# SBUF places of the matmul operands in both attentions of a two-block transformer kernel

## The chip, the cores and the metric

The kernel runs on one core of a Trainium2 chip. The metric is the device time in microseconds of one execution, taken as the median over several runs. The profile is one further look at one execution: its span runs from the first to the last instruction.

## The reference

The input is x, 32 sequences of 256 tokens and 256 channels in float32, and one condition vector of 256 a sequence. Two transformer blocks follow one another:

```python
# block 0 (film: scale and shift from cond)
h = film(rmsnorm(x, norm1_w), cond, film1_w, film1_b)
Q, K, V = h @ q_w + q_b, h @ k_w + k_b, h @ v_w + v_b      # one head of 256
x = x + softmax(Q @ K.T * D ** -0.5) @ V @ proj_w + proj_b
h = film(rmsnorm(x, norm2_w), cond, film2_w, film2_b)
x = x + gelu(h @ mlp_w1 + mlp_b1) @ mlp_w2 + mlp_b2          # 256 -> 1024 -> 256
# block 1 (shift, scale, gate from silu(c) @ w_ada + b_ada)
x_mod = ln(x) * (1 + scale_msa) + shift_msa
k, q, v = split(x_mod @ w_qkv)                              # 16 heads of 16
x = x + gate_msa * (attention(q / 16, k, v) @ w_proj + b_proj)
x_mod2 = ln(x) * (1 + scale_mlp) + shift_mlp
x = x + gate_mlp * (gelu(x_mod2 @ w_mlp1 + b_mlp1) @ w_mlp2 + b_mlp2)
```

## The kernel before

Four phases follow one another over all 32 sequences, with x held in SBUF throughout: A (attention of block 0), B (its MLP), C (attention of block 1), D (its MLP). Each phase is a software pipeline over the sequences, two of them a loop round, with the first and the last ones written out. Buffers with two copies are numbered 0 and 1 by the parity of the sequence; the profile leaves these numbers out.

**High and low parts.** Most products are taken on float32r operands in three steps. Every operand is split in a high part (rounded to float32r) and a low part (the rest), and `mm3` (from line 210) issues low times high, high times low and high times high into one accumulation. In the order of its arguments the first of a pair is the stationary operand, loaded as weights, and the second the moving one, which streams through the array. The profile names them the other way round: `bank<-a_h_hi,A_m_lo` moves a_h_hi over the stationary m_lo. Each such matmul has 128 stationary columns and 256 moving ones, both 4 bytes a column in each partition.

**Tokens.** `NormBuffers` (line 244) holds the normalized input of a sequence, transposed: `hi` and `lo`, two buffers of 2048 bytes a partition each. "a_" serves both attentions, "m_" both MLPs. Line 253 places the low ones right behind the high ones. Since both are a multiple of 2048 bytes, high and low start at the same place modulo 512.

**Attention A** (from line 451). For a sequence: the transposes of xhat (T, line 413); q (line 751) with the folded query-key weight m_hi, m_lo stationary and the tokens moving; v (line 762) with the tokens stationary and the folded value-projection weight vp_hi, vp_lo moving; S (scores, line 777) with the folded queries q_hi, q_lo stationary and the tokens moving; pT, the transposes of the probabilities (line 791); AV (line 795) with the transposed probabilities pT_hi, pT_lo stationary and v_hi, v_lo moving. q, v, S and AV are 12 matmuls each. The order on TensorE is set by due times in a table, modulo 16, and is in the steady state v, pT, T, S, AV, q, each task for a sequence of its own.

**Attention C** (from line 1507). q and k (`qk_cm`, line 1625) have weights stationary and tokens moving; v (line 1837) has tokens stationary and wt_v moving; the output projection PR (line 1828) has y_hi, y_lo stationary and wt_proj moving; each is 12 matmuls. Between them stand the scores of 16 heads (S0 to S7, line 1750, for the maxima; ST0 to ST7, line 1788, for exp), the weighted sums AV (line 1806) and transposes (lines 1816 and 1824). Every ST waits for the exp before it on ScalarE (line 1896). The order is again a table of due times.

**MLPs B and D** (from line 1017). up: w1 stationary, tokens moving, 48 matmuls a sequence. down: g (the activated hidden values, split) stationary, w2 moving, 48 matmuls.

**Places.** Tensors are placed by a stack allocator in the order of the calls, from the left end of SBUF upwards, or with side="right" from the right end downwards (the weights of B). The place of everything is thus set by the order of the calls and by unused tensors with names that begin with gap. LO_GAP is 32 elements (128 bytes): it stands between most high parts and their low parts. TOP_GAP (line 34) is the first thing on the right side, and so moves all of that side. `Weight.place` places high and low of a weight next to each other, `place_hi` and `place_lo` one of them. `L1Prep` (line 1353) places the weights of attention C.

Of the kernel before, what the change touches and what calls it, by code (L numbers as in the profile page):

```python
# [20 lines left out]
F32R = mybir.dt.float32r  # L21
# [3 lines left out]
P = 128  # L25
EPS = 1e-6
UNROLL = 2
PEEL = 10
X_FIRST = 4
SMALL = 24  # L30
W2_GAP, W2_SHIFT = 80, 48
Y_GAP = 32
GAP_BACK, GAP_BLOCKS = 4624, 1024
LO_GAP, TOP_GAP = 32, 56


class Seq:
# [61 lines left out]
def build(nc, a, out, mod_dram):  # L99


    NB, S, D = a["x"].shape
    TH, KT = S // P, D // P
# [7 lines left out]
    def allocator(stack, prefix):  # L111
        def sb(name, shape, dt=F32):
            return stack.enter_context(nc.sbuf_tensor(prefix + name, shape, dt))

        def ps(name, shape, dt=F32):
            return stack.enter_context(nc.psum_tensor(prefix + name, shape, dt))

        def sem(name):
            return semaphores.enter_context(nc.semaphore(prefix + name))

        def event(name, per=1, skip=0):


            if name in events:
                old = events[name]
                assert old.per == per
                events[name] = Event(old.sem, per, old.base + (NB - skip) * per)
            else:
                events[name] = Event(semaphores.enter_context(nc.semaphore("e_" + name)), per, -skip * per)
            return events[name]  # L130
        return sb, ps, sem, event

    with semaphores, root:
        sb, ps, sem, event = allocator(root, "")
# [2 lines left out]
        ident = sb("ident", [P, P])  # L137
        bank_pairs = [ps(f"bank{i}", [P, 1024]) for i in range(4)]
        banks = [pair[:, half:half + 512] for pair in bank_pairs for half in (0, 512)]
        small = {n: sb(n + "small", [P, SMALL]) for n in ("a_", "m_")}  # L140
        scale0m = sb("scale0m", [P, KT * NB])
        scale1a, shift1a = sb("scale1a", [P, KT * NB]), sb("shift1a", [P, KT * NB])
        rows = sb("rows", [P, 2 * D])
# [4 lines left out]
        class Weight:  # L148
# [3 lines left out]
            def __init__(self, sb, sem, name, view):  # L152
                self.view, self.t, self.N = view, view.shape[0] // P, view.shape[1]
                self.name, self.raw = name, None
                if sb:
                    self.place(sb)
                self.s_in, self.s_hi, self.s_lo = (sem(name + n) for n in ("_in", "_high", "_low"))
                self.s_read = sem(name + "_read") if name != "w2" else None
# [85 lines left out]
        class NormBuffers:  # L244

            def __init__(self, name):
                self.name = name
                t = small[name]
                self.stat, self.mv = t[:, 0:6 * TH], t[:, 6 * TH:8 * TH]
                self.var, self.msq, self.rstd = (t[:, TH * c:TH * (c + 1)] for c in (8, 9, 10))  # L250
                self.xhat = sb(name + "xhat", [P, TH * D])
                self.hi = [sb(f"{name}h_hi{u}", [P, KT * S], F32R) for u in range(UNROLL)]
                self.lo = [sb(f"{name}h_lo{u}", [P, KT * S], F32R) for u in range(UNROLL)]

        attention_norm, mlp_norm = NormBuffers("a_"), NormBuffers("m_")
        scale1m, consts = sb("scale1m", [P, KT * NB]), sb("consts", [P, 8])
        neghalf, one_rows, zero_col = consts[:, 0:TH], consts[:, TH:TH + 1], consts[:, TH + 1:TH + 2]

        BLOCK, QUADS = 32, P // 32
# [191 lines left out]
        def phase_l0_attention(mlp, start):  # L451
            with ExitStack() as st:
                sb, ps, sem, event = allocator(st, "A_")
# [8 lines left out]
                m_hi = sb("m_hi", [P, KT * D], F32R)  # L462
                sb("gap_mlo", [P, LO_GAP])
                m_lo = sb("m_lo", [P, KT * D], F32R)
                vp_hi, vp_lo = sb("vp_hi", [P, KT * D], F32R), sb("vp_lo", [P, KT * D], F32R)

                condT, actT = sb("condT", [P, KT * NB]), sb("actT", [P, KT * NB])
# [230 lines left out]
                def late_modulation(eng):  # L698
# [9 lines left out]
                        ins = add_bias(eng, pmod, 2 * slot, dst, b, lo, norm_w)  # L708
                    ins.then_inc(s_fix, 1)

                q_hi = sb("q_hi", [P, KT * S], F32R)
                sb("gap_q", [P, LO_GAP])
                q_lo = sb("q_lo", [P, KT * S], F32R)
                sb("gap_v", [P, LO_GAP])
                v_hi = [sb(f"v_hi{u}", [P, TH * D], F32R) for u in range(UNROLL)]
                v_lo = [sb(f"v_lo{u}", [P, TH * D], F32R) for u in range(UNROLL)]
                probs = [sb(f"probs{u}", [P, TH * S]) for u in range(UNROLL)]
# [631 lines left out]
        class L1Prep:  # L1349
# [3 lines left out]
            def __init__(self, sb, sem, sb_tmp, mlp):  # L1353
                self.mlp = mlp
                qkv = a["L1_cond_w_qkv"]
                self.w = {n: Weight(None, sem, n, v) for n, v in (("k", qkv[:, 0:D]), ("q", qkv[:, D:2 * D]),
                                                                ("v", qkv[:, 2 * D:3 * D]), ("proj", a["L1_cond_w_proj"]))}
                for n in "kq":
                    self.w[n].place_lo(sb)
                sb("gap_hi", [P, LO_GAP])  # L1360
                for n in "kq":
                    self.w[n].place_hi(sb)
                for n in ("v", "proj"):
                    self.w[n].place(sb)
                self.bias_q = sb("bias_q", [P, 2 * KT * NB])[:, 0:KT * NB]
                for w in list(self.w.values()) + mlp.w:
                    w.place_raw(sb_tmp)
                self.loaded = {n: mlp.w[0].raw[:, i * KT * D:(i + 1) * KT * D] for i, n in enumerate("qk")}
                self.cv, self.brow, mlp.b2row = (sb_tmp("next_" + n, s) for n, s in (
                    ("cv", [P, KT * NB]), ("brow", [NB, D]), ("b2row", [NB, D])))  # L1370
                sb_tmp("next_rest", [P, 448])
                self.blocks, self.back = sb_tmp("blocks", [P, TH * D]), sb_tmp("back", [P, TH * D])
                self.s_raw = {n: sem("raw_" + n) for n in "qk"}
                self.s_b, self.s_cv, self.s_g, self.s_out = (sem(n) for n in ("b", "cv", "g", "out"))
                self.s_one, self.s_zero = sem("one"), sem("zero")
                self.psum = banks[6]
                self.MLP_COL, self.PROJ_COL = 0, 256
                self.COL = {"v": 0, "q": 2 * NB}
# [774 lines left out]
        with near:  # L2153
            sb_near, sem_near = on_the_right(near, "B_")
            mlp0 = Mlp(0, sb_near, sem_near)
            shift1m = sb_near("shift1m", [P, KT * NB])
            mlp0.w.append(Weight(sb_near, sem_near, "w2", a["L0_cond_mlp_w2"]))
            with ExitStack() as early:
                start = Start(on_the_right(early, "Ap_")[0])
            with ExitStack() as raws:  # L2160
                for w in mlp0.w:
                    w.place_raw(on_the_right(raws, "B_")[0])
                heads["A"] = phase_l0_attention(mlp0, start)
            left = allocator(held, "C_")
            mlp1 = Mlp(1, *allocator(held, "D_")[::2])
            with ExitStack() as temps:
                prep = L1Prep(left[0], left[2], allocator(temps, "N_")[0], mlp1)
                heads["B"] = phase_mlp(mlp0, prep, heads["A"])
# [50 lines left out]
```

## Time and profile before

| | |
|---|---|
| time, three runs | 1575.3 us median (1571.78 to 1576.27) |
| profiled execution | span 1576.2 us, beside the longest of the three runs, 1576.27 |
| TensorE busy | 1528.6 us, 97% |
| VectorE, ScalarE, GpSimd busy | 1307.5, 869.0, 388.4 us |
| phase A | to about 265 us |
| phase B | about 300 to 600 us |
| phase C | about 600 to 1215 us |
| phase D | to the end |

Each matmul has a record with its start and a modelled end; one lasts some 280 ns in the records while the next starts after some 113 to 120 ns, since they are pipelined. So the busy time of TensorE says little of its speed, and the distance between two starts is what to read. The timeline gives starts to 0.01 us; over the 12 matmuls of a task that is about 1 ns a matmul.

### The profile page before, as it was taken

Reading aid. Unit: us, or ns where it says so; the run is one execution under the profiler, and the core shown is the slowest. Engines: PE = TensorE matmul, PEld = TensorE weight load, DVE = VectorE, ACT = ScalarE, POOL = GpSimd, SP = SyncE. Lnnn points to the kernel's source line nnn. Section 1 sums busy time; section 2 is a strip of 40 time slices with the busy share of each in tenths; the row PEclk is TensorE's granted clock in tenths of the full one; section 3 lists DMA queues with packets and bytes.
Section 4 is the critical chain, followed back from the end, with each engine's and each line's share of the span. In section 5 each row is a group of like instructions: output and inputs, shape, how many; then the busy total and the mean of one; then the engine's idle time right before and its main releaser. Section 6 shows DMA issues by size and latency. Waiting matters only on the chain.

```text
span 1576.2 us, 42177 instructions
## 1 busy us (share of the span) xinstructions
PE 1528.6 (97%) x14186; PEld 1373.0 (87%) x14186; DVE 1307.5 (83%) x2950; ACT 869.0 (55%) x1781; POOL 388.4 (25%) x525
## 2 busy tenths in 40 slices
PE   8999999999999998899999999999998999999999
PEld 7999998999999998677777777777775999999999
DVE  4788888777777787799999999999985888888886
ACT  3566664444444453566677766677665344444443
POOL 2343332010000013234344344443323200000000
PEclk9999999999999999899999999999998999999999
DMA  5700001211111111444344444443431233222332
GB/s 156 240 20 20 20 20 56 82 44 47 47 51 42 53 48 56 138 134 140 125 137 143 130 137 129 134 144 128 137 121 53 84 101 97 94 97 93 100 100 68
DMA packets 167665, 148.56 MB, mean 94 GB/s; under 512 B 24529, under 2 KB 146449, under 8 KB 167585
## 3 DMA queue, kind: packets, MB, share of 16 engines
q1 hardware_dynamic: 167424, 147.47, 29.3%
q8 instruction: 48, 0.79, 0.2%
q0 software_dynamic: 160, 0.04, 0.1%
q14 instruction: 33, 0.26, 0.1%
HBM read 62.61 MB, written 32.41 MB: 60 GB/s over the span
## 4 chain that ended last, share of the span: by engine, by line
PE 76%; issue 6%; DVE 5%; SPq 4%; DMA 4%; ACT 4%; DVEq 0%; ACTq 0%; POOL 0%; POOLq 0%
PE bank L216 58%; PE bank L1788 5%; PE bank L1806 4%; PE bank L1750 3%; ACT C_probs L1896 2%; DMA m_h_lo<-turned 2%; SPq L2102 2%; SPq L1690 2%; PE bank L1816 1%; PE bank L413 1%; PE bank L791 1%; DMA turned<-N_blocks 1%; PE bank L486 1%; PE bank L198 1%; DMA N_back<-turned 1%
## 5 line engine op out<-in xcount | busy, mean ns | idle before, releaser
L1896 ACT ACTIVATE C_probs<-bank 128x1024 f32<-128x1024 f32 x256 | 263.0, 1027 | 151.5 <-PE bank L1788 151.2
L1762 DVE TENSOR_REDUCE C_negmax<-bank 128x4 f32<-128x1024 f32 x248 | 303.6, 1224 | 30.4 <-PE bank L1750 24.1
L1127 ACT ACTIVATE D_g<-bank,D_bias 128x256 f32<-128x256 f32 x256 | 107.4, 472 | 198.2 <-PE bank L216 198.2
L1127 ACT ACTIVATE B_g<-bank,B_bias 128x256 f32<-128x256 f32 x256 | 107.4, 471 | 196.9 <-PE bank L216 196.8
L372 POOL TENSOR_TENSOR m_small<-m_small,consts 128x2 f32<-128x2 f32 x64 | 48.0, 750 | 592.0 <-DVE m_small L366 308.0
L1788 PEld LDWEIGHTS bank<-C_qs,C_kx 64*128 64x128 f32 x1024 | 77.9, 186 | 94.2 <-ACT C_probs L1896 61.2
L1788 PE MATMUL bank<-C_qs,C_kx 64*128 64x256 f32 x1024 | 130.3, 332 | 19.9 <-ACT C_probs L1896 19.8
L216 PE MATMUL bank<-B_wt_w_hi,B_g_lo 128*128 128x256 f32 x512 | 143.2, 280 | 3.7 <-DVE B_g_lo L1137 3.4
L216 PE MATMUL bank<-D_wt_w_hi,D_g_lo 128*128 128x256 f32 x512 | 141.8, 277 | 1.5 <-DVE D_g_lo L1137 1.5
L216 PE MATMUL bank<-m_h_hi,D_wt_w_lo 128*128 128x256 f32 x512 | 142.2, 278 | 0.8 <-DVE m_h_lo L432 0.8
L216 PE MATMUL bank<-m_h_hi,D_wt_w_hi 128*128 128x256 f32 x512 | 142.0, 277 | 0.0
L216 PE MATMUL bank<-m_h_lo,D_wt_w_hi 128*128 128x256 f32 x512 | 141.9, 277 | 0.0
L216 PE MATMUL bank<-m_h_hi,B_wt_w_lo 128*128 128x256 f32 x512 | 141.7, 277 | 0.0
L216 PE MATMUL bank<-B_wt_w_lo,B_g_hi 128*128 128x256 f32 x512 | 141.6, 276 | 0.0
L216 PE MATMUL bank<-B_wt_w_hi,B_g_hi 128*128 128x256 f32 x512 | 141.5, 276 | 0.0
L216 PE MATMUL bank<-D_wt_w_lo,D_g_hi 128*128 128x256 f32 x512 | 141.4, 276 | 0.0
L216 PE MATMUL bank<-D_wt_w_hi,D_g_hi 128*128 128x256 f32 x512 | 141.4, 276 | 0.0
L216 PE MATMUL bank<-m_h_lo,B_wt_w_hi 128*128 128x256 f32 x512 | 141.4, 276 | 0.0
L216 PE MATMUL bank<-m_h_hi,B_wt_w_hi 128*128 128x256 f32 x512 | 141.4, 276 | 0.0
L1806 PE MATMUL bank<-C_probs,C_vaug 128*32 128x256 f32 x2048 | 139.2, 390 | 0.0
L1750 PE MATMUL bank<-C_kx,C_qs 64*128 64x256 f32 x1024 | 115.9, 304 | 4.3 <-DVE m_xhat L1762 2.4
L1135 DVE CAST B_g_hi<-B_g 128x512 fp32r<-128x512 f32 x128 | 56.4, 440 | 65.6 <-ACT B_g L1127 65.1
(268 smaller groups left out, 4820.3 us busy)
## 6 DMA issues: line engine op xcount, KB each, us to landing
C_qs<-C_q_hi SPq DMA_DIRECT2D x128, 128.0 KB
C_kx<-C_k_hi SPq DMA_DIRECT2D x128, 128.0 KB, 2.6
C_qs<-C_q_lo SPq DMA_DIRECT2D x64, 128.0 KB
C_kx<-C_k_lo SPq DMA_DIRECT2D x64, 128.0 KB, 2.7
C_gbc<-mod_rows SPq DMA_DIRECT2D x32, 256.0 KB, 3.4
D_gbc<-mod_rows SPq DMA_DIRECT2D x32, 256.0 KB, 3.3
turned<-N_blocks SPq DMA_DIRECT2D x31, 256.0 KB, 2.0
N_back<-turned SPq DMA_DIRECT2D x124, 64.0 KB, 2.0
```

The source lines that it names most:

```text
L198: ins = eng.matmul(psum[:, col:col + NB], w.raw[:, k * w.N + c0:k * w.N + c0 + P], shift[:, k * NB:(k + 1) * NB], start=k == 0, stop=k == ...
L216: last = eng.matmul(out_ap, l, r, start=start and i == 0 and k == 0, stop=stop and i == n - 1 and k == 2, skip_group_check=skip)
L372: self.e_rstd.by(eng.tensor_tensor(self.rstd[:, :], self.var[:, :], neghalf[:, :], ALU.pow))
L1127: ins = eng.activation(o, p, func, bias=per_seq(bias1, 2 * u + d, b))
L1135: e_ghi.by(eng.tensor_copy(g_hi[u][:, :], g[u][:, :]))
L1690: eng.dma_start(half(stacked, b, w, slot), qk[f"{name}_{part}"][:, w * S:(w + 1) * S].bitcast(F32))\
L1750: ins = eng.matmul(spair[:, (e * TH + qh) * S:(e * TH + qh + 1) * S], qs[b.par][rows, t * S + qh:(t + 1) * S:TH], kx[b.par][rows, t * S:(t ...
L1762: e_max.by(eng.tensor_reduce(m4[:, :, :, j], spair[:, :].rearrange("p (e q k) -> p e q k", e=2, q=TH), AX, ALU.max, negate=True))
L1788: ins = eng.matmul(stpair[:, (e * TH + kh) * S:(e * TH + kh + 1) * S], kx[b.par][rows, t * S + kh * P:t * S + (kh + 1) * P], qs[b.par][row ...
L1806: ins = eng.matmul(ybank[32 * j:32 * j + 32, (g % 2) * S:(g % 2 + 1) * S], vaug[b.par][:, v0:v0 + 32], probs[h // 2 % NP][:, p0:p0 + S], s ...
L1896: e_exp.by(eng.activation(probs[t % NP][:, :], stpair[:, :], ACT.Exp, scale=scl))
L2102: eng.dma_start(half(qs, b, w, ROW_MAX)[:, :, quad * n:(quad + 1) * n], mT[w][p0:p0 + 16, :].bitcast(F32)).then_inc(s_md[w][b.par], 16)
```

## The change

Six edits, all on places. The calls that compute, wait or move data stay as they are, and so does their order.

- The small tensor `consts` moves to the front of the norm buffers, and unused tensors of 32 bytes take its old place and one new place: what follows lies 64 bytes further on.
- The low tokens of the attentions are placed before the high ones, in front of m_small.
- TOP_GAP grows from 56 to 168 elements: the right side moves down by 448 bytes.
- Attention A gets 256 bytes ahead of vp_hi, 512 ahead of q_hi, and 256 more ahead of v_hi.
- In attention C wt_v moves from behind wt_q_hi to behind wt_q_lo, with 256 bytes ahead of it; wt_proj comes after wt_q_hi without a gap, with 256 bytes behind it.

```diff
--- before.py
+++ after.py
@@ -31,7 +31,8 @@
 W2_GAP, W2_SHIFT = 80, 48
 Y_GAP = 32
 GAP_BACK, GAP_BLOCKS = 4624, 1024
-LO_GAP, TOP_GAP = 32, 56
+LO_GAP, TOP_GAP = 32, 168
+MOVING_GAP, Q_GAP = 64, 128
 
 
 class Seq:
@@ -137,7 +138,11 @@
         ident = sb("ident", [P, P])
         bank_pairs = [ps(f"bank{i}", [P, 1024]) for i in range(4)]
         banks = [pair[:, half:half + 512] for pair in bank_pairs for half in (0, 512)]
-        small = {n: sb(n + "small", [P, SMALL]) for n in ("a_", "m_")}
+        consts = sb("consts", [P, 8])
+        small = {"a_": sb("a_small", [P, SMALL])}
+        attention_lo = [sb(f"a_h_lo{u}", [P, KT * S], F32R) for u in range(UNROLL)]
+        small["m_"] = sb("m_small", [P, SMALL])
+        sb("gap_small", [P, 8])
         scale0m = sb("scale0m", [P, KT * NB])
         scale1a, shift1a = sb("scale1a", [P, KT * NB]), sb("shift1a", [P, KT * NB])
         rows = sb("rows", [P, 2 * D])
@@ -250,10 +255,12 @@
                 self.var, self.msq, self.rstd = (t[:, TH * c:TH * (c + 1)] for c in (8, 9, 10))
                 self.xhat = sb(name + "xhat", [P, TH * D])
                 self.hi = [sb(f"{name}h_hi{u}", [P, KT * S], F32R) for u in range(UNROLL)]
-                self.lo = [sb(f"{name}h_lo{u}", [P, KT * S], F32R) for u in range(UNROLL)]
+                self.lo = attention_lo if name == "a_" else [
+                    sb(f"{name}h_lo{u}", [P, KT * S], F32R) for u in range(UNROLL)]
 
         attention_norm, mlp_norm = NormBuffers("a_"), NormBuffers("m_")
-        scale1m, consts = sb("scale1m", [P, KT * NB]), sb("consts", [P, 8])
+        scale1m = sb("scale1m", [P, KT * NB])
+        sb("gap_consts", [P, 8])
         neghalf, one_rows, zero_col = consts[:, 0:TH], consts[:, TH:TH + 1], consts[:, TH + 1:TH + 2]
 
         BLOCK, QUADS = 32, P // 32
@@ -462,6 +469,7 @@
                 m_hi = sb("m_hi", [P, KT * D], F32R)
                 sb("gap_mlo", [P, LO_GAP])
                 m_lo = sb("m_lo", [P, KT * D], F32R)
+                sb("gap_vp", [P, MOVING_GAP])
                 vp_hi, vp_lo = sb("vp_hi", [P, KT * D], F32R), sb("vp_lo", [P, KT * D], F32R)
 
                 condT, actT = sb("condT", [P, KT * NB]), sb("actT", [P, KT * NB])
@@ -708,10 +716,11 @@
                         ins = add_bias(eng, pmod, 2 * slot, dst, b, lo, norm_w)
                     ins.then_inc(s_fix, 1)
 
+                sb("gap_qhi", [P, Q_GAP])
                 q_hi = sb("q_hi", [P, KT * S], F32R)
                 sb("gap_q", [P, LO_GAP])
                 q_lo = sb("q_lo", [P, KT * S], F32R)
-                sb("gap_v", [P, LO_GAP])
+                sb("gap_v", [P, LO_GAP + MOVING_GAP])
                 v_hi = [sb(f"v_hi{u}", [P, TH * D], F32R) for u in range(UNROLL)]
                 v_lo = [sb(f"v_lo{u}", [P, TH * D], F32R) for u in range(UNROLL)]
                 probs = [sb(f"probs{u}", [P, TH * S]) for u in range(UNROLL)]
@@ -1357,11 +1366,13 @@
                                                                 ("v", qkv[:, 2 * D:3 * D]), ("proj", a["L1_cond_w_proj"]))}
                 for n in "kq":
                     self.w[n].place_lo(sb)
+                sb("gap_v", [P, MOVING_GAP])
+                self.w["v"].place(sb)
                 sb("gap_hi", [P, LO_GAP])
                 for n in "kq":
                     self.w[n].place_hi(sb)
-                for n in ("v", "proj"):
-                    self.w[n].place(sb)
+                self.w["proj"].place(sb)
+                sb("gap_proj", [P, MOVING_GAP])
                 self.bias_q = sb("bias_q", [P, 2 * KT * NB])[:, 0:KT * NB]
                 for w in list(self.w.values()) + mlp.w:
                     w.place_raw(sb_tmp)
```

## Rows read from the trace of the kernel before

**Rows 1.** The page: span, and busy time of each engine.

```profile
span 1576.2 us, 42177 instructions
PE 1528.6 (97%) x14186; PEld 1373.0 (87%) x14186; DVE 1307.5 (83%) x2950; ACT 869.0 (55%) x1781; POOL 388.4 (25%) x525
```

**Rows 2.** Windows: length, busy us of PE PEld DVE ACT POOL, clock, DMA share, GB/s.

```profile
100.00:200.00 100.00, 100.00 (x860) 99.06 (x859) 88.56 (x248) 68.50 (x185) 33.25 (x47) 1.00 0.07 20
...
400.00:500.00 100.00, 100.00 (x885) 100.00 (x884) 76.85 (x184) 42.60 (x101) 6.20 (x9) 1.00 0.14 47
...
900.00:1000.00 100.00, 98.07 (x1053) 73.53 (x1052) 92.30 (x182) 71.72 (x119) 39.42 (x55) 1.00 0.44 138
```

**Rows 3.** Waits of PE from 100 to 250 us: total us, times, longest.

```profile
PE bank L216 <- DVE A_q_lo L858: 0.6, 1, 0.6
PE bank L791 <- ACT A_probs L840: 0.5, 1, 0.5
```

**Rows 4.** The chain that ended last, in B and D: start us, us, what.

```profile
347.80 204.45 PE bank L216 x1800
...
1230.95 341.37 PE bank L216 x3006
```

**Rows 5.** Timeline of PE in attention A: start us, us, instruction.

```profile
127.93 0.28 PE L216 MATMUL bank<-a_h_lo,A_q_hi 128*128 128x256 f32 x1
...
129.18 0.30 PE L216 MATMUL bank<-A_v_hi,A_pT_lo 128*128 128x256 f32 x1
...
130.61 0.28 PE L216 MATMUL bank<-a_h_hi,A_m_lo 128*128 128x256 f32 x1
...
133.41 0.60 PE L791 MATMUL bank<-ident,A_probs 128*128 128x128 f32 x4
...
134.56 0.28 PE L216 MATMUL bank<-a_h_lo,A_q_hi 128*128 128x256 f32 x1
...
135.82 0.28 PE L216 MATMUL bank<-A_v_hi,A_pT_lo 128*128 128x256 f32 x1
...
137.19 0.28 PE L216 MATMUL bank<-a_h_hi,A_m_lo 128*128 128x256 f32 x1
...
137.66 0.28 PE L216 MATMUL bank<-a_h_lo,A_m_hi 128*128 128x256 f32 x1
...
138.57 0.28 PE L216 MATMUL bank<-A_vp_hi,a_h_lo 128*128 128x256 f32 x1
...
139.99 0.60 PE L791 MATMUL bank<-ident,A_probs 128*128 128x128 f32 x4
140.42 0.60 PE L413 MATMUL bank<-ident,a_xhat 128*128 128x128 f32 x4
```

**Rows 6.** The same in attention C.

```profile
964.03 0.28 PE L216 MATMUL bank<-a_h_lo,C_wt_k_hi 128*128 128x256 f32 x1
...
965.21 0.28 PE L216 MATMUL bank<-a_h_hi,C_wt_k_hi 128*128 128x256 f32 x1
...
968.56 0.28 PE L216 MATMUL bank<-C_wt_v_lo,a_h_hi 128*128 128x256 f32 x1
...
969.86 0.60 PE L1824 MATMUL bank<-ident,C_ytok 128*128 128x128 f32 x4
...
975.64 0.28 PE L216 MATMUL bank<-C_wt_proj_lo,C_y_hi 128*128 128x256 f32 x1
...
976.81 0.28 PE L216 MATMUL bank<-C_wt_proj_hi,C_y_hi 128*128 128x256 f32 x1
```

**Rows 7.** Groups of PE's matmuls by form: count, busy us, mean ns of one.

```profile
L216 PE MATMUL bank<-C_wt_v_hi,a_h_lo 128*128 128x256 f32 x128 | 38.6, 302 | 0.3 <-DVE C_q_lo L1659 0.3
```

**Rows 8.** Waits from 952 to 988.1 us: total us, times, longest.

```profile
PEld bank L1788 <- ACT C_probs L1896: 3.3, 6, 0.8
```

**Rows 9.** The chain that ended last, in C: start us, us, what.

```profile
968.60 1.42 PE bank L216 x12
...
988.62 2.85 DMA m_h_lo<-turned
```

## The prediction

> **What bounds the kernel now.** I read the page first, then the same stretches by engine, then the chain, then single starts. On the page TensorE (PE) is busy for 97% of the span [rows 1]. By stretch, PE is busy for the whole of a 100 us window in the first attention and in the first MLP, and for 98 of 100 us in the second attention, at full granted clock [rows 2]. In the first attention, between 100 and 250 us, PE waits once for DVE (0.6 us) and once for ACT (0.5 us) [rows 3]. So the time of that attention and of the MLPs is a number of matmuls times the distance between two starts. I call that distance the pace. It is what this change could alter, since it adds, removes and reorders no instruction, wait or DMA.
>
> The MLPs give the pace to compare with. The chain shows 1800 matmuls of one line in 204.45 us and 3006 in 341.37 us, both 113.6 ns each [rows 4]. The attentions' projections have the same shape, 128 stationary columns and 256 moving ones. Their paces I take from starts in the timeline [rows 5, 6]:
> - First attention, v (138.57 to 139.99, 12 intervals): 118.3 ns.
> - q (137.19 to 138.57): 115.0 over all, of which the first four intervals (to 137.66) 117.5 and the other eight 113.8. So q opens slowly and then falls into the MLPs' pace.
> - Scores S (134.56 to 135.82, 11 intervals): 114.5; in the sequence before (127.93 to 129.18) 113.6. The attend step AV (135.82 to 137.19): 114.2, but 119.2 in the sequence before (129.18 to 130.61). So a task's pace also hangs on the state in which it is entered.
> - Second attention, v (968.56 to 969.86, 11 intervals): 118.2. k (964.03 to 965.21, 10 intervals): 118.0. The output projection (975.64 to 976.81, 10 intervals): 117.0.
>
> The whole prize: in the first attention the 47 intervals 127.93 to 133.41 take 5.48 us and those from 134.56 to 139.99 take 5.43, against 47 x 113.6 = 5.34. That is 0.115 us a sequence, 3.7 us for 32. In the second, v is 0.05 over, k 0.044, the output projection 0.034 at most and q not better known, say 0.12 together, 3.8 us for 32. No placement can bring more than 7.5 us, 0.5% of the time.
>
> **The change, part by part.** What differs is where operands start. I reduce each start modulo 512 bytes, since every slice used as an operand begins a multiple of 512 after its tensor's start. The starts follow from the declared sizes. I write M for the moving operand and W for the stationary one, and M-W for their distance.
>
> All of the left side moves on by 64 bytes (two added gaps of 32), later by 64 + 256 + 512 + 256 in the first attention and 64 + 256 + 256 in the second. The right side moves down by 448, which is also 64 modulo 512. So in both MLPs each M-W stays: 448 and 320 (up) and 192 and 64 (down) in the first, 192 and 64 in the second. I cost them at 0. A pace 1 ns worse over their 6144 matmuls would be 6 us, but 113.6 holds for all these distances [rows 4], and I know of no row in which a common shift of 64 matters.
>
> *Tokens.* High and low tokens start at the same place before, and 128 apart afterwards: from a_h_lo to a_h_hi there are now 4096 + 96 + 32 + 768 + 4096 bytes = 9088, or 384.
>
> *v projections.* There the tokens are the stationary operand. Before, consecutive weights start at the same place, M-W being 448 in the first attention and 64 in the second, all three products alike. It is the only one of the kernel's 256-column products whose high and low stationary operands coincide; everywhere else they are 128 apart. It is also the only one that is at 118 from its first interval to its last, in both attentions [rows 5, 6]. Afterwards M-W is 192 and 64 with weights 128 apart, as in the MLPs' down step, which runs at 113.6. I take it that v then settles as q does. It does not do so at once. Start places fall in two kinds, M an even and W an odd multiple of 64, or the reverse. The MLPs never change kind; AV to q changes it, and so does q to v, before and after. With four slow intervals as in q, eight of twelve gain 118.3 - 113.6 = 4.7 ns, 38 ns a sequence. Bounds: nothing, and 12 x 4.7 = 56 ns. The two v have 3 x 128 matmuls each [rows 7], 32 sequences: 1.2 us in the first attention (0 to 1.8) and the same on PE in the second.
>
> *q, S, k, q.* Here tokens move, and the three products get M-W 192, 320 and 64, where they had 192, 192, 64 (q), 448, 448, 320 (S) and 448, 448, 64 (both of the second attention). Each of these distances occurs in an MLP at 113.6, but no row has low moving data 128 on from high. Gain at best: what they lack, 3.8 us of the 7.5. Loss at worst: the pace 119.2 of the slow AV on all 48 matmuls a sequence, from 115.3 (q and S together; k and the other q are near it), 3.9 x 1536 = 6.0 us [rows 5]. I take 0, nearest to the four distances that all run well.
>
> *AV and output projection.* AV keeps 192 and 64; the output projection goes from 448 and 320 to 192 and 64. Both pairs run at 113.6 in an MLP: 0, the openings being bounded by 5 intervals x 4.7 ns x 64 = 1.5 us either way.
>
> *Transposes.* Identity stays while xhat, probs, ysb and ytok move by 64, so M-W for xhat and ytok goes from 64 to 0. Now four take 0.43 us, 108 ns each, for probs at another distance [rows 5]. 256 of them at 118 would cost 2.6 us; I take 0, since they stream 128 columns in that time and the matmuls twice as many.
>
> *What of the second attention's share reaches the end.* PE waits there 3.3 us by its weight loads for exp in one 36 us round [rows 8]. The chain of that round runs through one v (968.60, 12 matmuls), but at the other, 18 us later, it lies with the way to the turned tokens' DMA (2.85 us from 988.62) and not with PE [rows 9]. If that part sets the round, the second v's gain is given back as waiting. Half to all of 1.2: I take 0.9.
>
> Sum: 1.2 + 0.9 = 2.1 us. The profiled execution has a span of 1576.2, which lies 0.9 above the median of the three runs (1571.78 to 1576.27), so it is one of the longer ones; the same sum is taken off the median: 1575.3 - 2.1 = 1573.2 us.
>
> A rule that speaks against it: the Trainium skill, TensorE: Matmul & The Clock Gate, Step-by-step: what each phase is for, says that TensorE has two independent SBUF read ports, and that "loading the next tile's weights doesn't steal SBUF read bandwidth from the running matmul". By it places don't matter and the time stays at 1575.3. The trace does not settle it: it has two paces for one shape, which the rule doesn't foresee, but no row shows the same product at two places.
>
> **The rivals.**
> (a) All openings go too, and the attentions run at 113.6 throughout: 7.5 us less, 1567.8. For it: 3006 matmuls in a row keep that pace while up and down alternate [rows 4]. Against: transposes and score matmuls stand between the attentions' tasks, and the two kinds stay mixed.
> (b) Places do nothing, and v is slow by what goes before it: 1575.3. For it: AV's 114.2 and 119.2 at places that differ only by whole multiples of 512. Against: v is slow after q, and after transposes in the second attention, alike.
> (c) Slower: the low tokens as moving data, 128 on, keep q, S, k and q from settling, as the coincidence keeps v. The place is these 1536 matmuls; at 120 ns, 4.7 more than 115.3, it costs 7.2 us, less 2.1 gained in v: 1575.3 + 5.1 = 1580.4. It decides from 116.7 ns on, where 1.4 x 1536 eats the 2.1. For it: nothing else in the kernel has this arrangement, so no row vouches for it. Against: each distance on its own runs well.
>
> **How the numbers follow.** Forecast 0.46, (a) 0.20, (b) 0.15, (c) 0.19. A measurement of this kernel tells about 0.3% (4.7 us) from no change, so faster means under 1570.6 and slower over 1580.0. Faster: nearly all of (a), 0.19, and 0.12 of the forecast's case where S and k settle as well: 0.31. Slower: 0.13 of (c) and 0.02 for the transposes and the MLPs' shift: 0.15. The rest, 0.54, is the same. The range reaches past (a), as the runs scatter by 4.5 us, and past (c): 1567.0 to 1581.0. The likeliest case alone: 1570.5 to 1576.
>
> **What would show it.** In the timeline after, v should open with some four intervals of 118 to 120 ns and go on at 113 to 114 in both attentions: 1.38 us or so from v's first start to the transposes, not 1.42. If v takes 1.42 again, coincidence was not its cause (b). The first attention's q and S must keep 1.38 and 1.26; 1.44 is (c). Both MLPs must keep 113.6. A round of the second attention lasts 36 us and should lose 0.05 to 0.08; if v gets faster there and the round doesn't, exp or the DMA sets it. I am wrong as a whole if the time moves by more than 5 us either way.

## The result and the profile after

| | before | after |
|---|---|---|
| time, median of 20 runs each | 1573.35 us (1570.51 to 1577.26) | 1578.1 us (1574.68 to 1581.26) |
| ratio | | 1.0026, 95% interval 1.0017 to 1.0034 |
| profiled execution, span | 1576.2 us | 1573.2 us |

The change makes the kernel slower by 0.26%, some 4.1 us (2.7 to 5.3; the two medians are 4.75 us apart), where 2.1 us less was forecast. The profiled execution after is one of the shorter ones, the one before one of the longer: the two spans alone would show the wrong sign. What differs between them lies in the first sequences of A and in the last ones of B and C, which scatter by 1 to 3.5 us even between two executions of one kernel (e7 and e14 below: 1.3 us at the first q of A, 3.5 us from the end of A to the first k of C). So the traces are compared by their paces in the steady part.

The page of the changed kernel, span and busy time. Against [rows 1] nothing moves by more than 0.2%.

```profile
span 1573.2 us, 42177 instructions
PE 1528.5 (97%) x14186; PEld 1373.7 (87%) x14186; DVE 1309.6 (83%) x2950; ACT 870.5 (55%) x1781; POOL 388.6 (25%) x525
```

Windows of the changed kernel (columns as in [rows 2]). In the first attention TensorE is just as full and at full clock, but gets through 851 matmuls in 100 us where it had 860, 1.0% fewer; in the MLP it has the same 885, and in the second attention 1052 for 1053.

```profile
100.00:200.00 100.00, 100.00 (x851) 99.09 (x850) 88.06 (x242) 68.03 (x184) 32.82 (x47) 1.00 0.07 20
400.00:500.00 100.00, 100.00 (x885) 100.00 (x884) 77.00 (x184) 42.70 (x102) 6.22 (x9) 1.00 0.14 47
900.00:1000.00 100.00, 98.19 (x1052) 73.66 (x1050) 92.69 (x182) 71.00 (x117) 40.29 (x55) 1.00 0.43 135
```

TensorE's waits of the changed kernel from 100 to 250 us are the same two as in [rows 3], so the missing matmuls aren't waiting for anyone:

```profile
PE bank L221 <- DVE A_q_lo L867: 0.5, 1, 0.5
PE bank L800 <- ACT A_probs L849: 0.5, 1, 0.5
```

Timeline of TensorE in A of the changed kernel (start us, us, instruction), answering [rows 5]: second matmul of S, first of AV, of q, the fifth of q, first of v, then the transposes.

```profile
132.91 0.28 PE L221 MATMUL bank<-a_h_lo,A_q_hi 128*128 128x256 f32 x1
...
134.21 0.28 PE L221 MATMUL bank<-A_v_hi,A_pT_lo 128*128 128x256 f32 x1
...
135.62 0.28 PE L221 MATMUL bank<-a_h_hi,A_m_lo 128*128 128x256 f32 x1
...
136.09 0.28 PE L221 MATMUL bank<-a_h_lo,A_m_hi 128*128 128x256 f32 x1
...
137.03 0.29 PE L221 MATMUL bank<-A_vp_hi,a_h_lo 128*128 128x256 f32 x1
...
138.46 0.49 PE L800 MATMUL bank<-ident,A_probs 128*128 128x128 f32 x3
...
138.89 0.49 PE L420 MATMUL bank<-ident,a_xhat 128*128 128x128 f32 x3
```

S takes 1.30 us for its 11 intervals (118.2 ns; before 114.5), AV 1.41 for 12 (117.5; before 114.2), q 1.41 (117.5; before 115.0) and v 1.43 (119.2; before 118.3). q opens with four intervals in 0.47 us as before, but the other eight take 0.94, 117.5 ns, where they took 113.8. The 47 intervals from S to the transposes take 5.55 us; before it was 5.48 and 5.43.

In C of the changed kernel, answering [rows 6]: k from its second to its last start, v from its second start to the transposes.

```profile
962.52 0.29 PE L221 MATMUL bank<-a_h_lo,C_wt_k_hi 128*128 128x256 f32 x1
...
963.70 0.28 PE L221 MATMUL bank<-a_h_hi,C_wt_k_hi 128*128 128x256 f32 x1
...
967.05 0.28 PE L221 MATMUL bank<-C_wt_v_lo,a_h_hi 128*128 128x256 f32 x1
...
967.41 0.28 PE L221 MATMUL bank<-C_wt_v_lo,a_h_hi 128*128 128x256 f32 x1
...
967.64 0.28 PE L221 MATMUL bank<-C_wt_v_hi,a_h_lo 128*128 128x256 f32 x1
...
968.34 0.49 PE L1835 MATMUL bank<-ident,C_ytok 128*128 128x128 f32 x3
```

k takes 1.18 us for 10 intervals as before. v takes 1.29 us for 11 where it took 1.30: it opens at 120 ns (0.36 us for the three from 967.05) and has 117 in the last six (0.70 us from 967.64).

The chain of the changed kernel in B and D (start us, us, what), answering [rows 4]: 234.64 / 2064 = 113.7 ns and 274.61 / 2418 = 113.6. The MLPs' pace is what it was.

```profile
337.69 234.64 PE bank L221 x2064
...
1294.64 274.61 PE bank L221 x2418
```

**All starts together.** The table is worked out from every start in a trace: the mean distance between two matmuls of one task in ns (those under 150), and in brackets what all of them take over 113.3 ns each, in us for the whole phase. 113.3 is the pace of a task that has settled, as I call it when it has come down and stays there. The step from a task's last matmul to the next task isn't counted. The kernels e1 to e8 are told of below.

```
        before        after         e3 (after)    e1            e2            e7            e8
A q     115.2 (0.64)  117.8 (1.55)  117.8 (1.56)  117.8 (1.55)  115.3 (0.68)  115.2 (0.64)  117.8 (1.55)
A v     117.7 (1.54)  118.0 (1.65)  117.9 (1.58)  118.1 (1.66)  117.8 (1.55)  117.7 (1.55)  118.0 (1.64)
A S     116.5 (1.03)  118.0 (1.49)  118.2 (1.55)  118.1 (1.53)  117.0 (1.20)  116.8 (1.11)  118.1 (1.54)
A AV    115.1 (0.63)  116.6 (1.13)  116.6 (1.13)  116.3 (1.04)  114.7 (0.48)  114.4 (0.39)  116.4 (1.06)
C k     116.7 (1.07)  117.7 (1.38)  117.8 (1.38)  117.7 (1.38)  115.6 (0.73)  115.3 (0.63)  117.7 (1.38)
C q     114.7 (0.45)  117.7 (1.41)  117.8 (1.45)  118.1 (1.53)  116.9 (1.16)  116.6 (1.06)  117.8 (1.45)
C v     117.9 (1.48)  117.2 (1.21)  116.8 (1.09)  115.7 (0.78)  114.5 (0.36)  114.6 (0.40)  116.6 (1.03)
C PR    115.9 (0.81)  115.3 (0.63)  115.7 (0.74)  115.7 (0.74)  115.5 (0.69)  116.2 (0.90)  115.7 (0.74)
sum            7.64         10.45         10.49         10.21          6.84          6.69         10.40
us of 22 sequences in A's loop
        143.64        145.19        145.20        145.10        143.65        143.52        145.17
us of C's loop
        396.55        395.77        396.10        396.37        396.20        395.81        396.98
```

e3 is the changed kernel once more, and repeats its means to 0.4 ns: the paces belong to the kernel and not to the execution. Two executions of e7's kernel (e7 and e14) differ in one task by up to 0.9 ns (C's q, 0.30 us) and in the sum by 0.09 us. C's k and q scatter most: they take 1.07 and 0.45 us before, and 0.76 and 0.87 in e4, which has the same distances. With the last step of each task counted the sums are 8.34 us before and 11.06 after, 2.7 us apart instead of 2.8.

A's loop grows by 1.55 us in 22 sequences; scaled to 32 that is an estimate of 2.25 us. C's loop doesn't grow, though k and q in it do: TensorE isn't what sets a round there [rows 8, 9]. So the traces account for some 2.3 us of the 4.1 (2.7 to 5.3) measured; the second measurement of the same kernel gave 2.5 (0.5 to 4.6). What is left, 0.4 to 3 us, I can't place, because the written-out first and last sequences scatter by more.

### The profile page after: what moved, and what is told of

Read it like the earlier page. It is cut to its first block, busy times and chain, and to the rows that moved or that the text cites. A ratio compares the mean times of both kernels' runs of the same rounds, so it can differ in the third digit from the quotient of the medians.

```text
span 1573.2 us, 42177 instructions
## 1 busy us (share of the span) xinstructions
PE 1528.5 (97%) x14186; PEld 1373.7 (87%) x14186; DVE 1309.6 (83%) x2950; ACT 870.5 (55%) x1781; POOL 388.6 (25%) x525
## 4 chain that ended last, share of the span: by engine, by line
PE 80%; issue 5%; DVE 5%; ACT 4%; DMA 3%; SPq 2%; DVEq 0%; ACTq 0%; POOL 0%; POOLq 0%
PE bank L221 59%; PE bank L1799 6%; PE bank L1817 6%; PE bank L1761 4%; ACT C_probs L1907 2%; PE bank L1827 2%; PE bank L420 1%; PE bank L800 1%; DMA m_h_lo<-turned 1%; PE bank L1835 1%; PE bank L494 1%; SPq L1701 1%; ACT C_y_f L1925 1%; SPq L2113 1%; ACT C_y_hi L1924 1%
```

## The experiments

Each was a change of places alone, unless its diff says otherwise. Distances (a, b, c) are, modulo 512: a, how many bytes further on the high moving operand starts than the high stationary one; b, the low moving one than the high stationary; c, the high moving one than the low stationary.

**Which part costs.** e1 has the changed kernel's tokens, the low ones 128 on, while weights, folded queries and v_hi keep their distances to the high tokens as before; e2 is the changed kernel with the low tokens back at the place of the high ones; e4 is the kernel before with everything moved by 64; e3 is the changed kernel once more.

```diff
 e1, against the changed kernel
-                sb("gap_vp", [P, MOVING_GAP])
-                sb("gap_qhi", [P, Q_GAP])
-                sb("gap_v", [P, LO_GAP + MOVING_GAP])
+                sb("gap_v", [P, LO_GAP])
...
 e2, against the changed kernel
-        attention_lo = [sb(f"a_h_lo{u}", [P, KT * S], F32R) for u in range(UNROLL)]
...
-                self.lo = attention_lo if name == "a_" else [
-                    sb(f"{name}h_lo{u}", [P, KT * S], F32R) for u in range(UNROLL)]
+                self.lo = [sb(f"{name}h_lo{u}", [P, KT * S], F32R) for u in range(UNROLL)]
 e4, against the changed kernel: both of these
```

> Of the change only the low tokens' place (128 on from the high ones) and the common shift of 64; weights, folded queries and value weights keep the distances of before. Theory L (low tokens 128 on as the moving operand keep q, S, k and q from settling): q of the first attention at 118 ns (12 intervals 1.41 us, before 1.38), S at 118, both of the second attention at 118, so it is as slow as the changed kernel, +0.2% on before. Theory D (the distances that the change gave weights and queries do it, 320 for the low tokens on the high weights): q of the first attention has the changed kernel's distances and is at 118, S has 448, 64, 320 and settles at 113 to 114. Theory N (the slowdown is not in TensorE's pace): paces as before, time as before.

> The changed kernel with the low tokens behind the high ones again, at the same place modulo 512. Every product but v then has M-W 192, 192, 64, as the last MLP's. Theory L: q, S, k and q settle at 113 to 114 within the first third of the task, AV is entered settled; v stays at 118 throughout, its stationary operands coinciding. Time 3 to 5 us below the changed kernel, 0 to 2 us below before. Theory D: the distances of weights and queries are kept, so q and S stay at 118 and the time is the changed kernel's. Theory N: no pace changes.

> Before, with everything that holds a matmul operand 64 bytes on modulo 512 and no distance between operands altered (only identity and x stay). Theories L and D: paces of every task as before (first attention q 115, v 118, S 114 to 117, AV 114 to 119), time within 0.15% of before. Theory N (a shift as such costs, or the transposes, whose distance to identity goes to 0): transposes above 109 ns or MLPs above 113.6, and +0.2%.

> The changed kernel unaltered, a second profiled execution. If the paces are a property of the places, q, S, k, q and v show the same interval at the same position of the loop as in the first profile, to 1 ns; if they drift with the execution, the two profiles differ there. Time 0.2 to 0.35% over before.

Measured, with 95% intervals: e1 1.0017 (1.0005 to 1.0029), e2 0.9989 (0.9977 to 1.0001), e4 1.0003 (0.9987 to 1.0018), e3 1.0016 (1.0003 to 1.0029). The low tokens' place carries the slowdown: with it e1's paces in q, S, k and C's q are those of the changed kernel, without it e2's are not, and the intervals of e1 and e2 lie apart. Modulo 512, e1 differs from e4 in this place alone. Timeline of e1: first q, first v.

```profile
128.97 0.28 PE L221 MATMUL bank<-a_h_hi,A_m_lo 128*128 128x256 f32 x1
...
130.38 0.29 PE L221 MATMUL bank<-A_vp_hi,a_h_lo 128*128 128x256 f32 x1
```

The same of e4:

```profile
133.46 0.28 PE L220 MATMUL bank<-a_h_hi,A_m_lo 128*128 128x256 f32 x1
...
134.84 0.28 PE L220 MATMUL bank<-A_vp_hi,a_h_lo 128*128 128x256 f32 x1
```

q takes 1.41 us in e1 and 1.38 in e4 (117.8 and 115.2 ns in the mean over all sequences), though the intervals of the two whole times overlap.

The common shift does nothing that stands clear of the scatter: e4's sum over the eight tasks is 7.53 us, beside 7.64 before. One v of C in e2 (start us, us, instruction; second, fourth, seventh start, transposes):

```profile
946.98 0.28 PE L220 MATMUL bank<-C_wt_v_lo,a_h_hi 128*128 128x256 f32 x1
...
947.22 0.28 PE L220 MATMUL bank<-C_wt_v_hi,a_h_lo 128*128 128x256 f32 x1
...
947.56 0.28 PE L220 MATMUL bank<-C_wt_v_hi,a_h_lo 128*128 128x256 f32 x1
...
948.24 0.49 PE L1833 MATMUL bank<-ident,C_ytok 128*128 128x128 f32 x3
```

From 947.22 to 948.24 it has 9 intervals of 113.3 ns, though its high and low stationary tokens coincide modulo 512 as they do in the kernel before. So coincidence of the stationary operands, the cause that the forecast named, is not enough to keep v slow in C. (The moving operands start 192 on from the coinciding ones here, and 64 before.) Of A's v this says nothing; it runs at 117.8 in e2.

**Late or never?** In e5 (changed) and e6 (before) q, v and S of A are issued three times in a row, 36 matmuls instead of 12, the same result.

```diff
-                        for t in range(KT):
+                        for t in [*range(KT)] * 3:
```

> The changed kernel with the 12 matmuls of q, of v and of S of the first attention each issued three times over into the same bank (36 in a row, the result the same), to see where a task's pace goes if it is given time. Theory L, strong form (low tokens 128 apart as moving data never settle): q and S stay at 118 over all 36, while v, whose distances are those of the MLPs' down step, is at 113 to 114 from about the 12th on. Theory O (the opening is only longer): q and S are at 113 to 114 in their last 12.

> The same threefold issue in the kernel before. Theory V (coincident high and low stationary operands keep v from settling, as my prediction had it): v at 118 over all 36. Theory O: v is at 113 to 114 in its last 12, so that in the kernel before too it only lacked time. q and S at 113 to 114 in the last 24 by either.

Timeline of e5: first q, first v, eighth v, transposes, second S, first AV.

```profile
150.20 0.28 PE L221 MATMUL bank<-a_h_hi,A_m_lo 128*128 128x256 f32 x1
...
154.44 0.28 PE L221 MATMUL bank<-A_vp_hi,a_h_lo 128*128 128x256 f32 x1
...
155.28 0.28 PE L221 MATMUL bank<-A_vp_lo,a_h_hi 128*128 128x256 f32 x1
...
158.57 0.49 PE L800 MATMUL bank<-ident,A_probs 128*128 128x128 f32 x3
...
159.56 0.28 PE L221 MATMUL bank<-a_h_lo,A_q_hi 128*128 128x256 f32 x1
...
163.69 0.28 PE L221 MATMUL bank<-A_v_hi,A_pT_lo 128*128 128x256 f32 x1
```

The same of e6: first q, the fifth, first v, transposes, second S, first AV.

```profile
151.12 0.28 PE L216 MATMUL bank<-a_h_hi,A_m_lo 128*128 128x256 f32 x1
...
151.60 0.28 PE L216 MATMUL bank<-a_h_lo,A_m_hi 128*128 128x256 f32 x1
...
155.23 0.28 PE L216 MATMUL bank<-A_vp_hi,a_h_lo 128*128 128x256 f32 x1
...
159.47 0.49 PE L791 MATMUL bank<-ident,A_probs 128*128 128x128 f32 x3
...
160.47 0.28 PE L216 MATMUL bank<-a_h_lo,A_q_hi 128*128 128x256 f32 x1
...
164.45 0.28 PE L216 MATMUL bank<-A_v_hi,A_pT_lo 128*128 128x256 f32 x1
```

With the low tokens 128 on, 36 matmuls of q take 4.24 us, 117.8 ns each to the end, and S 4.13 us for 35, 118.0. In the kernel before q takes 4.11 us, 0.48 for the first four and 3.63 for the other 32, 113.4 each, and S 3.98, 113.7. v is the reverse: 4.24 us throughout before, 117.8 ns, while after it has 120 ns for seven intervals and then 3.29 us for 29, 113.4. So q and S don't settle late, they don't settle at all; and with the changed places v can settle, here from its eighth interval on. In the changed kernel itself, where v has twelve matmuls and is entered from a shorter q, it doesn't get there: its intervals 8 to 12 are some 118, 120, 118, 114 and 116 ns (medians over the sequences). The whole times, 1831.25 and 1833.39 us, are one run each and tell nothing at this size.

**Which distance of the low tokens?** e7 puts them 256 on, e8 384 on. e14 is e7 again.

```diff
 e7, against the changed kernel
-        attention_lo = [sb(f"a_h_lo{u}", [P, KT * S], F32R) for u in range(UNROLL)]
         small["m_"] = sb("m_small", [P, SMALL])
         sb("gap_small", [P, 8])
+        attention_lo = [sb(f"a_h_lo{u}", [P, KT * S], F32R) for u in range(UNROLL)]
```

> The changed kernel with the low tokens 256 instead of 128 on from the high ones. Theory L (what counts is that high and low moving data start at different places): q, S, k and q of the second attention stay at 118, time as the changed kernel, +0.15 to 0.25% on before. Theory D (what counts is the distance 320 of the low tokens from the high weights, here 448): they settle at 113 to 114, time 3 us below the changed kernel.

> The changed kernel with the low tokens 384 on from the high ones; their distance to the high weights is 64. Theory L: 118 as in the changed kernel. Theory D: 113 to 114 after the opening.

> The changed kernel with the low tokens 256 on instead of 128, once more. By the sum over the tasks 0.95 us under the kernel before; its ten runs so far gave a ratio of 0.9983 (0.9965 to 1.0001). All theories: a ratio between 0.9985 and 1.0; if the interval ends under 1 it beats the kernel before.

Timeline of e7: first q, the fifth, first v.

```profile
134.74 0.28 PE L221 MATMUL bank<-a_h_hi,A_m_lo 128*128 128x256 f32 x1
...
135.22 0.28 PE L221 MATMUL bank<-a_h_lo,A_m_hi 128*128 128x256 f32 x1
...
136.12 0.28 PE L221 MATMUL bank<-A_vp_hi,a_h_lo 128*128 128x256 f32 x1
```

q opens in 0.48 us and has 0.90 for the other eight, 113 ns. In e8 it stays at 117.8. e7 measured 0.9983 (0.9965 to 1.0001), and again 0.9994 (0.9981 to 1.0006); e8 1.0002 (0.9985 to 1.0019), though its paces are those of the changed kernel. So its time alone would not show the slowdown; what counts here is the paces, and A's loop of 145.17 us. Together: with 0 or 256 between the moving high and low tokens A's q and C's k settle in every sequence, while S of A and C's q, at 116.6 to 117.0 ns in the mean, come down late in one sequence of two. With 128 or 384 none of the four settles. So it isn't any difference between the two that does harm, and not the distance 320 alone either (e8 has 64 in its place).

**The moving operands' distance from one another, or from the weights?** e10: low tokens together with the high ones, and the stationary operands of A's q and S moved by 128, distances (64, 64, 448).

```diff
 e10, against e2
+                sb("gap_mhi", [P, 32])
                 m_hi = sb("m_hi", [P, KT * D], F32R)
...
-                sb("gap_qhi", [P, Q_GAP])
+                sb("gap_qhi", [P, Q_GAP + 32])
```

> Low tokens at the place of the high ones modulo 512, as before; in attention A the stationary operands of q and S are moved by 128 bytes, so that high and low moving tokens are each 64 on from the high stationary part (192 before in q, 448 in S), and 448 from the low one. So far q, S, k and q of C did not settle (118 ns over all twelve) wherever the low tokens stood 64 or 320 on from the high stationary part, which was also wherever they stood 128 or 384 from the high tokens. Theory M-M (only the distance of the two moving operands from one another counts): q and S of A settle, 115.2 to 117 ns in the mean, with 113 at the end of q. Theory M-W (64 or 320 from moving to high stationary is what keeps the pace up): q and S of A stay at 118 over all twelve. Attention C is as in the kernel with the low tokens together, in both.

Timeline of e10: first q, first v; second S, first AV.

```profile
128.50 0.28 PE L220 MATMUL bank<-a_h_hi,A_m_lo 128*128 128x256 f32 x1
...
129.91 0.28 PE L220 MATMUL bank<-A_vp_hi,a_h_lo 128*128 128x256 f32 x1
...
138.91 0.28 PE L220 MATMUL bank<-a_h_lo,A_q_hi 128*128 128x256 f32 x1
...
140.16 0.32 PE L220 MATMUL bank<-A_v_hi,A_pT_lo 128*128 128x256 f32 x1
```

q: 1.41 us for 12, 117.5 (mean 118.3 over all sequences). S: 1.25 for 11, 113.6 (114.6). One and the same set of distances, and q never settles while S does at once. Neither theory holds: the moving operands' distance from one another isn't all, and (64, 64, 448) isn't bad by itself.

e13 has these distances in S alone.

> The kernel with the low tokens together with the high ones modulo 512, and q_hi, q_lo alone moved by 128 bytes, so that S of A has the distances 64, 64, 448, while q of A keeps 192, 192, 64. With weights and folded queries both at 64, q ran at 118.3 and S at 114.6 (116.5 in the kernel before, 117.0 with 192). Theory places: S runs at 114.6 here as well, 0.7 to 0.8 us less than with 192, and q at 115.2: a sum over the eight tasks of about 6.1 us over 113.3, 1.5 us under the kernel before, so 1573.8 beside 1575.3. Theory entry (S ran well there since what stands before it was in another state): S stays at 116 to 117, and the sum at 6.8.

S ran at 117.1, 0.2 us slower than in the kernel before over the phase and not faster: in every second sequence it opened 117 116 114 and then stayed at 113 to 114 (medians over the sequences), in the others it went on at 118 with a 124 among them. After an S that has settled AV runs at 113 to 114 from its second interval, after the other kind it stays at 116 to 122 for eight, at the same places. What stands before S decides too, so e10's good S was not its places' doing alone. For q the pair says more: e10 and e13 differ in the place of q's weights alone, and q runs at 118.3 and 115.3. The time was 1572.29 us, ratio 0.9982 (0.9969 to 0.9995): the only kernel whose interval ends below 1. Its sum over 113.3 is 7.01 us, 0.6 less than before, which is a fifth of the 2.8 us that the ratio says, and A's loop takes 144.05 us, 0.4 more than before. So its paces don't explain its time. e7's first ratio moved from 0.9983 to 0.9994 when it was measured again, and e13 was measured once; its gain may be chance.

**Why does v of A stay slow?** e11 is e2 with q, v and S thrice. e9 is e7 with v moved behind the transposes pT, so that it comes out of transposes as in C; e12 is e9 with the PSUM banks of v and S exchanged.

```diff
 e9, against e7 (hi_v and lo_v follow, at 39 and 40.5)
-                T_PE = {"T": 22, "S": 39, "AV": 58, "q": 30, "v": 33, "pT": 52.5}
+                T_PE = {"T": 22, "S": 39, "AV": 58, "q": 30, "v": 37, "pT": 52.5}
 e12, against e9
-                bT, bQ, _, bV, bS, bPT, bR, pmod = banks
+                bT, bQ, _, bS, bV, bPT, bR, pmod = banks
```

> The changed kernel with the low tokens at the place of the high ones modulo 512, and in attention A the matmuls of q, v and S issued three times in a row (36 each, the same result). The stationary tokens of v coincide modulo 512, and v's moving operands are 192 from both. Theory coincidence (the prediction's: stationary high and low at one place keep v of A slow, and 36 matmuls don't help): v stays at 118 to the end, as it did in the kernel before with 36. Theory distance and entry (448 held v of the kernel before up; 192 lets it settle, only later than in C, since it comes straight out of q): v reaches 113 between the eighth and the thirtieth. q and S settle in both, and stay at 113.

> The low tokens start 256 bytes on from the high ones, and in attention A the task v is moved from behind q to behind pT, in front of T (its high and low parts follow on ScalarE and VectorE). In every kernel so far v of A ran at 118 ns a matmul over all twelve, while v of C with the same distances to its weights (192, 192, 448) settled from the fourth on, at 114.6 ns in the mean. Theory entry (what goes before a task decides too; v of A comes straight out of q, v of C out of transposes): v of A now opens like v of C, 122 116 114 113, and takes about 114.6 to 115 ns in the mean; 12 x 3 ns x 32 sequences = 1.2 us less than with v behind q, 1573.2 beside a kernel before of 1575.3 less 2.7. Theory buffers (v of A is slow for what it reads and writes, wherever it stands): v stays at 118, and the time stays within 0.3 us of the kernel with 256 bytes between the tokens and v behind q. What the task does to q and pT, which now follow one another, goes with both: up to 0.3 us a sequence more if pT has to wait for exp, 10 us in all, and then there is a gap ahead of pT in the timeline of TensorE.

> The kernel with v behind pT and the low tokens 256 on, and in attention A the PSUM banks of v and S exchanged (v writes bank 4, S bank 3); places in SBUF, order and waits as there. Theory bank (the place of the output decides whether a task settles: v of A wrote bank 3 in every kernel and ran at 118 in every one but one, while v of C, at the same places modulo 16384 bytes, settled at once): v of A opens 122 116 114 113 and runs at about 114.6 ns in the mean, and S, now in bank 3, stays at 118, so the two about cancel. Theory not the bank (something else of A, such as what the other engines read and write beside it): v stays at 118 over all twelve and S settles as before, 115.8 in the mean.

Timeline of e11: first v, transposes.

```profile
153.30 0.28 PE L220 MATMUL bank<-A_vp_hi,a_h_lo 128*128 128x256 f32 x1
...
157.55 0.49 PE L798 MATMUL bank<-ident,A_probs 128*128 128x128 f32 x3
```

Of e9: second v, transposes of xhat behind it.

```profile
133.18 0.28 PE L221 MATMUL bank<-A_vp_lo,a_h_hi 128*128 128x256 f32 x1
...
134.48 0.49 PE L420 MATMUL bank<-ident,a_xhat 128*128 128x128 f32 x3
```

e11: 4.25 us for 36, 118.1 to the end. e9: 1.30 for 11, 118.2. e12: 117.6 in the mean of all, as e9. The same product at the same places (vp_hi in A and wt_v_hi in C lie exactly 16384 bytes apart, with the same stationary tokens) runs at 118 in A and at 114.5 in C. In A that holds after q and after transposes (e7, e9) and in two PSUM banks (e9, e12). In e11 the distances were (192, 192, 192) and v never settled; with (192, 192, 64) in e5 it did. So for A's v the forecast's theory of coincidence stands as far as the runs with 36 matmuls go: it never settles in e6 and e11, where the stationary operands coincide, and does in e5, where they don't. e7 and e9, with 256 between them, gave it twelve matmuls only. Why A's v doesn't come down within twelve as C's does stays open; what other engines read and write beside it was not varied. e9 measured 1.002 (1.0006 to 1.0033), slower, though its sum is the least of all, 5.72 us, and its loop in A the shortest, 143.12 us: moving v costs something outside the loop. From the start of the last q but one to the end of AV there are 18.75 us in e9 and e12, and 18.14 in e7; the rest I haven't placed. e12's one run gave 1576.23 us.

## Why the prediction was wrong

- **The bound.** Right: TensorE's pace is the only thing that moved, waits and clock stayed, and in C part of a change of pace doesn't reach the end. It reached it even less than "half to all": C's loop stayed within 1.2 us in all seven traces of the table, and is no longer after than before.
- **q, S, k, q: "I take 0, nearest to the four distances that all run well".** This is the step that failed, and the term that turned the sign. The tasks lost 0.91 + 0.46 us in A and 0.31 + 0.96 in C, 2.64 us; against e4 in place of the kernel before, C's two lost 0.62 and 0.54. Each distance does run well in an MLP; the moving high and low operands being 128 apart does not, and the forecast had noted that no row has this arrangement. That was rival (c)'s mechanism, its price set at 120 ns; they ran at 117.7 to 118.0, above its deciding 116.7. Its 5.1 us more is near the 4.1 measured partly by luck: it charged the four tasks 7.2 us and gave 2.1 back in v, where the traces show 2.64 us, another 0.50 in AV and next to nothing back.
- **AV, 0 with 1.5 us of openings as a bound.** It lost 0.50 us, inside the bound: S now hands over unsettled, and AV, whose places are as before, needs about eight intervals to reach 113. The cost of a task that doesn't settle falls partly on the next.
- **v: "I take it that v then settles as q does", 1.2 us in each attention.** Failed as to the cause and the size. In A the pace went from 117.7 to 118.0 and cost 0.11 (with the step into the transposes counted v gained 0.11); it didn't settle in its twelve matmuls, and with 36 of them, in e5, from the eighth interval and not the fifth. In C it gained 0.27. Coincidence was not what kept C's v slow: e2 and e7, with stationary operands 0 and 256 apart, let it settle from the fourth on, at 114.5, faster than 128 apart. For A's v it isn't ruled out (e6, e11). Four slow intervals as in q was a hopeful choice too: k's 118.0 over ten intervals, in the forecast's own rows, tells of a longer opening at places that it counted as good.
- **Output projection, transposes, the common shift of the MLPs: 0.** Right: -0.18 us; four transposes take 0.43 us (138.46 to 138.89) as before; 113.6 to 113.7. e4 shows the shift alone.
- **Rivals (a) and (b).** (a), that all openings go, did not come: they stayed or spread. (b), that places do nothing, fails in q (e1 against e4). It is right for A's v in its number, not in its reason: e9 changed what goes before v, and v stayed.
- **The rule on the two read ports** (the Trainium skill, TensorE: Matmul & The Clock Gate, Step-by-step: what each phase is for: loading weights takes no SBUF bandwidth from the running matmul). By it e2 and e1 would run alike, and e10 and e13 too. They differ by 2.5 and 3.0 ns a matmul in q. So a matmul's pace depends on its operands' places, by up to the 4% between 113.3 and 118; that the weight load takes read bandwidth is a guess that no run here shows.

Sum of the eight tasks: +2.8 us instead of -2.4.

## What to carry to other kernels

A distance between operands that runs well in one product vouches for that distance and not for a new arrangement: where both pieces of a new pattern are known and the pattern isn't, its bounds belong in the forecast and not its zero. When moving operands alternate between two buffers, 0 or 256 bytes apart modulo 512 is worth a try before 128 or 384; it was better in four tasks of this kernel, and e10's q shows that it doesn't suffice. And when a change is one of pace, compare the steady loops' starts: one span against another had the wrong sign here, and the median of 20 runs was needed.

## What the runs showed of the hardware

- One shape (128 stationary columns, 256 moving ones, float32r) has two paces at full granted clock, 113.3 and 118 ns, and a task can stay at the slow one for all of 36 matmuls (e5's q, e6's v) or at the fast one for the last 32 (e6's q). The change from the slow to the fast one often goes 122, 116, 114, 113 over four intervals; the state is handed to the next task (AV of e13, by the S before it).
- Places modulo 512 don't fix it: v of A and v of C at equal places differ (117.8 and 114.5 in e2), q and S of e10 differ at equal distances (118.3, 114.6), and so does S of e13 from one sequence to the next.
- The exchange of PSUM banks left the pace of v as it was, 117.6 (e9, e12).
